# Down's low product by 26 block products over four output chunks, in place of 28 by pairs

## The reference

```python
gate = einsum('bsh,mh->bsm', y, W_gate)      # W_gate, W_up: 3584 x 1024
up   = einsum('bsh,mh->bsm', y, W_up)
h    = silu(gate) * up
out  = x + einsum('bsm,hm->bsh', h, W_down)  # W_down: 1024 x 3584
```

## Time and profile before

| | us |
|---|---|
| median of 3 runs (lowest to highest) | 1321.77 (1321.36 to 1321.96) |
| the profiled execution's own time | 1321.53 |
| its span, first to last instruction | 1319.7 |
| TensorE busy | 1313.9 |
| VectorE busy | 798.7 |
| ScalarE busy | 405.2 |
| GpSimd busy | 118.6 |

### The profile page before, as it was taken

One profiled execution on the slowest core, in us unless ns is written; L12 is line 12 of the kernel. 1 busy time (PEld: TensorE's weight loads), 2 busy tenths in 40 slices (PEclk: granted clock), 3 DMA queues, 4 the chain that ended last, 5 costly groups with the idle time before them and its releaser, 6 DMA issues.

```text
span 1319.7 us, 22220 instructions
## 1 busy us (share of the span) xinstructions
PE 1313.9 (100%) x8592; PEld 863.0 (65%) x8592; DVE 798.7 (61%) x1529; ACT 405.2 (31%) x703; POOL 118.6 (9%) x156
## 2 busy tenths in 40 slices
PE   9999999999999999999999999999999999999999
PEld 7854566546666666676667666667666766666666
DVE  7889898788525577763733455555473254545623
ACT  4387756461102343421101233332110122222000
POOL 3200011150001011100000111110000011111000
PEclk9999999999999999999999999999999999999999
DMA  8379987216946688843784668553387456566564
GB/s 296 152 271 361 368 288 257 76 63 241 346 147 185 253 314 323 321 142 113 275 299 156 224 204 275 180 156 121 113 314 266 135 185 184 180 180 216 165 233 136
DMA packets 119609, 287.58 MB, mean 218 GB/s; under 512 B 15184, under 2 KB 18896, under 8 KB 118736
## 3 DMA queue, kind: packets, MB, share of 16 engines
q1 hardware_dynamic: 119216, 285.99, 63.2%
q10 hardware_dynamic: 288, 0.16, 0.0%
HBM read 241.80 MB, written 44.30 MB: 217 GB/s over the span
## 4 chain that ended last, share of the span: by engine, by line
PE 99%; DVE 1%; DMA 0%; issue 0%; DVEq 0%; ACTq 0%
PE banks L1072 26%; PE banks L1025 23%; PE banks L1095 14%; PE banks L1102 13%; PE banks L815 4%; PE banks L993 3%; PE banks L994 3%; PE banks L867 2%; PE banks L911 1%; PE banks L913 1%; PE banks L912 1%; PE banks L908 1%; PE banks L910 1%; PE banks L909 1%; PE banks L1131 1%; PE banks L751 1%
## 5 line engine op out<-in xcount | busy, mean ns | idle before, releaser
L1072 PE MATMUL banks<-y_hi,gu_ring 128*128 128x512 f16 x1552 | 365.3, 379 | 0.0
L1072 PEld LDWEIGHTS banks<-y_hi,gu_ring 128*128 128x128 f16 x1552 | 151.9, 98 | 143.4
L1095 PE MATMUL banks<-h,piece 128*128 128x512 f16 x840 | 188.5, 379 | 0.0
L2274 POOL TENSOR_TENSOR m<-m,m 128x256 f32<-128x256 f32 x100 | 72.7, 727 | 820.7 <-DVE m L1740 815.2
L2033 ACT ACTIVATE sg<-banks,sc 128x512 f32<-128x512 f32 x112 | 76.7, 687 | 225.6 <-DVE banks L1759 164.0
L1095 PEld LDWEIGHTS banks<-h,piece 128*128 128x128 f16 x840 | 82.2, 98 | 89.7
L1762 DVE TENSOR_TENSOR banks<-banks,m 128x256 f32<-128x256 f32 x100 | 43.2, 432 | 134.8 <-PE banks L1072 134.6
L1102 PE MATMUL banks<-h,piece 128*128 128x256 f16 x896 | 106.1, 273 | 0.0
L1102 PEld LDWEIGHTS banks<-h,piece 128*128 128x128 f16 x896 | 87.7, 98 | 19.7
L1025 PE MATMUL banks<-y_lo,gu_ring 128*128 128x256 f16 x776 | 100.5, 273 | 0.0
L2161 ACT COPY m<-banks 128x256 f32<-128x256 f32 x100 | 36.9, 369 | 170.4 <-PE banks L1025 170.2
(11 more groups left out here) (257 smaller groups left out, 1997.3 us busy)
## 6 DMA issues: line engine op xcount, KB each, us to landing
piece<-down_dram SPq DMA_DIRECT2D x80, 448.0 KB, 5.6
mix_c<-mix_dram SPq DMA_DIRECT2D x84, 384.0 KB, 4.0
piece<-Wd SPq DMA_DIRECT2D x64, 448.0 KB, 5.3
gu_ring<-Wg SPq DMA_DIRECT2D x108, 256.0 KB, 3.3
gu_ring<-Wu SPq DMA_DIRECT2D x108, 256.0 KB, 3.0
mix_a<-mix_dram SPq DMA_DIRECT2D x84, 256.0 KB, 2.7
mix_dram<-mixed SPq DMA_DIRECT2D x28, 640.0 KB, 5.4
wb<-w_dram SPq DMA_DIRECT2D x64, 256.0 KB, 3.3
```

The source lines that it names most:

```text
L1072: mm = MM(bank, w[:, k, :], y_hi[:, k, :], start=False, stop=(k == KC - 1), skip_group_check=True)
L1095: mm = MM(bank, w[:, k, :], h[:, half * MH + k, 0, :], start=(start and k == 0), stop=False, skip_group_check=True)
L2274: G.tensor_tensor(m1[:, n % 3], m1[:, n % 3], m32[:, n % 2], ALU.add).then_inc(s_1236, 1)
```

## The change

Down's low product is done for four output chunks at a time (GROUP = 4, two groups g = 0, 1), by blocks of 1 chunk x 7 chunks of the inner side x 256 columns: 4 x 4 x 2 blocks, 26 products instead of 32, each done for both groups one after the other with the same h (`product`). A piece of `down_dram` now holds one product's weights of both groups, 2 x 7 blocks. A batch has 42 pieces instead of 36: 8 raw ones of group 0, 26 of products, 8 raw ones of group 1. The high product of group 0 comes first, then all of the low product, then the high product of group 1.

```diff
+    LOWS_AT = (9, 2, 11, 10, 13, 4, 18, 25, 8, 6, 1, 16, 5, 12, 3, 7, 22, 21, 20, 17, 15, 24, 19, 14, 23, 26)
+    HIGHS = 2 * GROUP
+    BATCH_PIECES = PRODUCTS + 2 * HIGHS
-    SPLIT_W = {4: 0, 18: 1, 19: 2}
+    SPLIT_W = {4: 0, 20: 1, 21: 2}
-    LOAD_W = {2: 0, 16: 1, 17: 2}
-    PLAIN = 12
+    LOAD_W = {2: 0, 18: 1, 19: 2}
+    PLAIN = 14
+    WD_PART = {3 + 7 * g + i: (g, i) for g in range(2) for i in range(7)}
+            def product(b, p, i, j, y, first=False, keeps=None, nodes=None):
+                w = piece(b, HIGHS + low_at(p))
+                for g in range(2):
+                    if first and g:
+                        pe.wait_ge(s_oh, GROUP * b + i)
+                    if keeps:
+                        pe.wait_ge(s_kept, kept(b, keeps, g))
+                    if nodes:
+                        pe.wait_ge(s_node, node(b, nodes, g))
+                    for k in range(QUARTER):
+                        mm = MM(low_half(g, i, j), w[:, QUARTER * g + k, :], y[:, k, :], start=(first and k == 0),
+                                stop=False, skip_group_check=True)
+                    mm.then_inc(s_piece if g else s_low, 1)
+            def down_low(b):
...
+                product(b, 9, 1, 2, h_block(1, 2), first=True)
+                product(b, 2, 2, 2, h_block(3, 2), first=True)
+                product(b, 11, 4, 2, h_block(2, 1), first=True)
+                product(b, 10, 4, 1, h_block(1, 1), keeps="v10")
+                product(b, 13, 3, 1, sums(b, "n3"), first=True)
...
+                product(b, 22, 1, 1, sums(b, "n1"), keeps="v6")
...
+                product(b, 15, 1, 1, hs["n7"], nodes="v1")
```

`keeps` names a copy by ScalarE that must be out of the bank before the product is added onto it (v10 is the copy of product 11), `nodes` a sum by VectorE. Per batch ScalarE makes 26 copies of 256 columns, VectorE 22 sums of such copies and banks into a running result `acc`, GpSimd 24 adds between them:

```diff
+                for g in range(2):
+                    multiplied(b, 11, g)
+                    S.copy(acc_half(g, 4, 1), low_half(g, 4, 2)).then_inc(s_kept, 1)
...
+                for g in range(2):
+                    pool.wait_ge(s_kept, kept(b, "v8", g))
+                    gather(acc_half(g, 1, 1), acc_half(g, 1, 1), tmp[g][0][:], ALU.subtract)
...
+                for g in range(2):
+                    multiplied(b, 22, g)
+                    dve.wait_ge(s_kept, kept(b, "v8", g))
+                    dve.wait_ge(s_part, part(b, "c11", g))
+                    V.tensor_tensor(tmp[g][0][:], low_half(g, 1, 1), tmp[g][0][:], ALU.subtract).then_inc(s_node, 1)
```

In batch 0 the weights' sums ("nodes") are 28 for each group, 128 x 896 elements, four in each of the units 3 to 16, formed partly in place in the loaded rows and stored at once (`wd_nodes` on VectorE, `store_wd` on SyncE, in place of `down_weight_sum` and `store_down_sum`):

```diff
+            def wd_nodes(g, i):
...
+                elif i == 3:
+                    dve.wait_ge(s_dhalf, 8 * g + 6)
+                    V.tensor_tensor(w(1, 1), w(1, 1), w(1, 3), ALU.add).then_inc(s_dnode, 1)
+                    V.tensor_tensor(w(3, 3), w(3, 3), w(1, 3), ALU.subtract).then_inc(s_dnode, 1)
+                    V.tensor_tensor(wd_slot[4][:], w(1, 3), wd_slot[0][:], ALU.add).then_inc(s_dnode, 1)
+                    V.tensor_tensor(w(1, 3), w(1, 3), w(3, 4), ALU.subtract).then_inc(s_dnode, 1)
```

```diff
+                    elif j == 20 and b + 1 < NB:
                         for s in range(1, GU_SLOTS):
                             load_gu(MC * (b + 1) + s)
+                    elif j == 30:
+                        load_xr(b, 1)
+                for i in range(GROUP):
+                    store(b, i)
                 if b + 1 < NB:
+                    sp.wait_ge(s_fin, GROUP * (b + 1))
```

More of the change, by code:

```diff
@@ L39 @@
 EARLY_W = 3
-WD_SUMS = 4
 WORK = 3
@@ L503, in load_a, with wd_stored, stored @@
+            def wd_stored():
+                for i in range(3):
+                    sp.wait_ge(d_slot[i], (128, 32, 160)[i])
+                for i in range(3):
+                    sp.wait_ge(d_row[i], (256, 128, 128)[i])
+            def stored(b):
+                if b:
+                    sp.wait_ge(d_out, 16 * OC * b)
             def load_a(i):
@@ L729, in _ @@
+            b = NB - 1
+            for i in range(GROUP, OC - 1):
+                store(b, i)
+            sp.wait_ge(s_oh, GROUP * NB + 1)
+            sp.dma_start(outT[b, :, OC - 1, 0:HALF], o_sb[:, OC - 1, 0:HALF]).then_inc(d_out, 16)
+            sp.wait_ge(s_o, OC * NB)
+            sp.dma_start(outT[b, :, OC - 1, HALF:T], o_sb[:, OC - 1, HALF:T]).then_inc(d_out, 16)
+            sp.wait_ge(d_out, 16 * (OC * NB + 1))
         @block.tensor
@@ L1125, in down @@
+            def down(b):
+                for c in range(GROUP):
+                    if b + 1 == NB:
+                        pe.wait_ge(s_sg, MC * NB - 2)
+                        pe.wait_ge(s_hf, MC * NB - 2)
+                    elif b + 1 >= FINE and c == 2:
                         pe.wait_ge(s_yc, OC * (b + 1) + 6)
                         pe.wait_ge(s_yfix, fixed(b + 1, 6))
-                    w = piece(b, j)
-                    if q == 0:
+                    bank = banks[:, c, :]
+                    w = piece(b, 2 * c)
+                    if c == 0:
@@ new lines, in down @@
+                    down_high(bank, piece(b, 2 * c + 1), 1).then_inc(s_piece, 1)
+                down_low(b)
+                n = MC * (b + 1)
+                for c in range(GROUP):
+                    bank = banks[:, GROUP + c, :]
+                    j = HIGHS + PRODUCTS + 2 * c
+                    pe.wait_ge(s_node, node(b, ("o11", "o22", "o31", "o41")[c], 0))
+                    if b + 1 < NB:
+                        down_high(bank, piece(b, j), 0).then_inc(s_piece, 1)
+                        if c == 2:
+                            products_12(n)
+                        elif c == 3:
+                            products_34(n)
+                            products_12(n + 1)
+                        down_high(bank, piece(b, j + 1), 1).then_inc(s_piece, 1)
+                        if c == 3:
+                            products_576(n)
+                    elif c < GROUP - 1:
+                        down_high(bank, piece(b, j), 0).then_inc(s_piece, 1)
+                        down_high(bank, piece(b, j + 1), 1).then_inc(s_piece, 1)
+                    else:
+                        first, second = piece(b, j), piece(b, j + 1)
+                        for half in range(2):
+                            at = slice(half * HALF, (half + 1) * HALF)
+                            for k in range(MC):
+                                w = (first if k < MH else second)[:, k % MH, :]
+                                mm = MM(banks[:, (OC - 1, 0)[half], at], w, h[:, k, 0, at], start=(k == 0), stop=False,
+                                        skip_group_check=True)
+                            mm.then_inc(s_piece, 1)
```

791 lines of the change are left out of this document (502 added, 289 removed).

## The result

| | before | after |
|---|---|---|
| median, lowest to highest (us) | 1321.77 (1321.36 to 1322.12, 7 runs) | 1316.91 (1315.52 to 1317.64, 7 runs) |
| the profiled execution | 1321.53, span 1319.7 | 1316.32, span 1314.5 |

The ratio is 0.9961, 95% interval 0.995 to 0.9972: faster by 4.9 us, where 7.2 were forecast. The profiled executions differ by 5.21 us.

The account below looks back on a forecast made before the run. TensorE's matmul pace plus its waits was taken as the bound. -12.24 + 0.08 + 0.79 + 4.5 - 0.3 = -7.2 us gave a median of 1314.6 us, range 1310.3 to 1318.8 (forecast's own 1312.5 to 1317).

Parts of the forecast that it names:

- two plain units, last chunk in halves: Batch 0's units 12 and 13 done the plain way, +0.79 us; batch 3's last chunk of down cut in halves, +0.08.
- the seam: Batch 0's switch from plain to block units: VectorE late for y's differences; TensorE stalls 1.05 us, then 0.43.
- four sums at units 13 to 16: Batch 0's block units: four weight sums a unit take VectorE 2.3 us, up to 1.91 free; stalls of 2.65 us.
- W on x: Batch 0: splitting W moves from units 18 and 19 to 20 and 21, onto x's splits; 0.85 us of stalls.
- stalls of before: The old kernel's two TensorE waits in batch 0's gate/up, 0.28 and 0.22 us, subtracted as 0.50.
- the end, from the last matmul's start: Kernel's end: the last drain and its store no longer wait behind others, -0.3 us (0 to -0.6).
- Queue and DMA in batch 0. Cost 0: Batch 0's larger stores and SP's 56 issues delay nothing: 0 us, a few if the 20 us of cover went.
- Down itself. Cost 0, at most 2 us: In down, copies, adds, sums of h and the next batch's weights all come in time: 0, at most 2 us.
- The third rival: Down's low product: weight pieces arrive too late and it is slower, about 1349 us; chance 0.06.
- VectorE keeps up: Rival: in batch 0, sums are shorter or overlap more, only the seam is left; 1311.1 us, chance 0.13.
- GpSimd's adds: Rival: in down's low product they exclude VectorE's sums, +1 to +2 us a batch, about 1320; chance 0.10.
- More VectorE lag: Rival: weight sums take VectorE 2.8 us a unit instead of 2.3, and a unit more to drain; 1318, chance 0.09.

Follow-up runs that it names:

- e8: Changed kernel with gate/up loads issued apart, plus low block products 23 and 26 issued twice (112 matmuls more): 1326.65 us.
- e11: Kernel before, with batch 0's start of units by blocks moved from unit 12 to 14 and the changed kernel's list of gate/up weight sums: 1322.53 us.
- e4: Changed kernel with ScalarE's two copies for the next products put ahead of a pair's first silu in batch 0's block units: 1315.82 us.
- e2: Changed kernel with 16 of VectorE's weight sums at units 13 to 16 of batch 0 made on 4 columns in place of 896: 1313.55 us.
- e5: Changed kernel with gate/up loads issued apart, and three weight sums at each of units 13 to 16, four at 17: 1318.31 us.
- e7: Changed kernel with gate/up loads issued apart, and GpSimd's 24 adds per batch in the low product made on 4 columns, not 256: 1313.9 us.
- e12: Kernel of e5 with the next batch's x loaded in four parts behind units 18 to 21's gate/up loads, and W as in e9: 1313.25 us.
- e9: Changed kernel with gate/up loads issued apart, and the next batch's W chunks loaded at units 21, 22 and split at 24, 25: 1313.4 us.
- e3: Changed kernel with the parts of the weight sums packed into units 3 to 13 in place of one in each of units 3 to 16: 1324.46 us.
- e6: Kernel of e5 with two sums at unit 13, three at 14 to 17, two at 18, and x and W loads and splits one unit later: 1328.74 us.

## Why the prediction was right, and by how much not

| step | forecast | in the profile |
|---|---|---|
| 112 low matmuls fewer | -12.24 | -12.24 (e8: 12.05) |
| two plain units, last chunk in halves | +0.87 | +0.87 (e11: 0.98) |
| the seam | +1.48 | 1.79 + 0.41 = +2.20 |
| four sums at units 13 to 16 | +2.65 | 0.32 + 0.38 + 1.38 + 0.38 = +2.46 |
| W on x | +0.85 | 0.21 + 0.37 + 0.25 + 0.17 = +1.00 |
| stalls of before | -0.50 | -0.50 |
| the end, from the last matmul's start | -0.3 | 2.97 for 3.46: -0.49 |
| down | 0, at most 2 | +1.53 |
| sum | -7.19 | -5.17 (measured -5.21) |

- The time came out 2.3 us above the forecast, and 0.1 inside its own narrower range (to 1317). One of its signs of being wrong did show, idle TensorE in down behind a piece's DMA: the mechanism held for the large terms, and two terms that it put at nothing cost 0.9 and 1.5 us.
- The price of an 896-element add was right: 617 ns, starts 0.54 us apart. So was the way from VectorE's free time to the stalls: 1.38 for 1.54, 0.32 for 0.35. Two stalls it had put to VectorE (0.38 each) are shown as ScalarE's, whose copies stand behind a silu that waits for VectorE's `complete`; e4 shows it is the same lag.
- "Queue and DMA in batch 0. Cost 0" is one step that failed. No load held TensorE, as forecast, but a store held VectorE: a slot's, issued at 144.83 and landed at 151.00, for which VectorE stood still for 1.94 us. The walk of SyncE's queue priced loads behind stores and not the reuse of the stores' buffers. The forecast had VectorE at the differences of y at 165.4; it came at 166.09. That is 0.7 of the missing 2.0 us. Where the wait is under 0.9 us the stall is 0.86 and not the 1.05 of the forecast, so the wait cost 0.93 us, and the seam's own term was 0.2 too high.
- "Down itself. Cost 0, at most 2 us" is the other. The third rival had seen the place ("the one behind the burst of gate/up weights has 1.9 us to spare"), but that margin did not hold. The piece took 7.6 us where the page's median landing was 5.6, and SyncE needed 3.1 us (3.6 in batch 0) for the six issues ahead of it; TensorE stood 0.2 to 0.7 us for it. Of the 1.53 us, 0.24 stand behind the loads of x, a burst that the rival counted in its bytes and not in its margins. Its price as a rival (+10 us in a batch) was far off all the same: from 340 to 375 us the DMAs moved 371 GB/s, well over the 311 from which it decides.

```profile
340.00:375.00 35.00, 34.90 (x319) 30.83 (x317) 25.67 (x36) 7.72 (x21) 23.14 (x24) 1.00 1.00 371
```

- The end gained 0.2 more than forecast: the last drain (1311.88) starts behind nothing.
- "It waits in two places only" left out the kernel's start: the kernel before has some 2 us of small stalls in its first 60 us. The change left that about as it was (the 200th matmul starts at 41.89 before and 41.83 after).
- Of the rivals, "VectorE keeps up" fell by e2 and e5, and "GpSimd's adds" by e7: the exclusion is there, and the sums of h that it lengthens have that much room. What spoke against it was misread: the 727 ns are gate and up's adds, 726 in the changed kernel too, while down's take 937. "More VectorE lag" did not come: the block units cost 2.46 us for 2.65.
- Still open: why the slot's store lands up to 2.1 us late in one execution and in time in another with the same code, and the small stalls in the kernel's start, which no edit here touches. Not tried: storing the slot's sum sooner or using another slot, and the loads of x at piece 30 apart.

The best version is e12 or e9, 1313.25 and 1313.4, not to be told apart: some 3.5 us below the changed kernel, 8.2 below the one before. Their remaining stalls in batch 0 (3.5 and 3.7 us) come from VectorE's lag. Each has one late load besides: 0.59 us in e9 (above), and in e12 0.50 at 802.49, where blocks for gate and up, issued at 793.94 behind twelve loads of `wb`, landed at 802.44.

## What to carry to other kernels

When work on the fast engine gets shorter, ask of every queue whether its tightest item, and not its mean, still arrives: put bursts of loads where the consumer is slow, and not ahead of the item it waits for. An in-order engine that makes data for stores waits for the stores' buffers too, and a load that must wait for "all stored" holds what is queued behind it. Free time counts only where it stands in the engine's order: sums moved ahead by up to three units made this kernel 7.6 us slower.

## What the runs showed of the hardware

- After TensorE had stood for 8.66 us in e3, the first matmuls of 512 columns started 0.43 us apart instead of 0.216, which is the clock's lower level of 1.2 GHz; the stretch's granted clock was 0.66. The matmuls at that level took some 2.5 us longer. In e6 the same came behind a stall of 2.70 us (227.04): matmuls of 256 columns then started 0.214 us apart, and the granted clock from 226 to 231 was 0.66. In e5's profiled execution a stall of 2.44 us (221.7) left the clock at 1.00, but seven of its eleven runs have a granted clock of 0.997 to 0.999, and they are the seven slowest.
- Pieces of the same 448 KB took 3.3 to 8.6 us to land in down of batch 1 of the changed kernel (3.3 for those issued at 650.03 and 656.07, 8.6 for the one issued at 670.03 behind the burst). A median of the page says little of the one transfer that something waits for.
- VectorE's wait for one slot's store differs by 2.1 us between executions whose code is the same up to there (0 to 2.08): the same store took 4.3 to 6.3 us to land. All of the wait beyond 0.9 us shows as a stall of TensorE, less 0.15.
